# A gated cross-attention and expert layer on one core: the token work between the path walk and the softmax loop in one pass, or in four tiles of 112 tokens

## The chip, the core and the metric

The kernel runs on one core of a Trainium2 chip. The core has TensorE (PE: matrix products into the PSUM banks, and the loading of their weights), VectorE (DVE), ScalarE (ACT: activation functions with a table each), GpSimd (POOL) and SyncE (SP, which issues transfers). Each takes its own instructions in order and waits on semaphores for the others. The metric is the device time of one execution in microseconds. "Before" was run three times.

## The reference

`x` has 8 batches of 56 tokens with 128 features (448 tokens), the context 8 batches of 1500 rows. Four layers follow each other, each added to `x` with a factor `tanh(g)`:

```
x = x + tanh(g_xattn[0]) * align(context, layernorm(x))          # dynamic time warping
x = x + tanh(g_ffn[0])   * product_key_memory(layernorm(x))      # 8 heads, 1 expert each
x = x + tanh(g_xattn[1]) * attention(layernorm(x), context)      # 16 heads of 8
x = x + tanh(g_ffn[1])   * experts(layernorm(x))                 # 8 experts, best 2
```

`align` computes all distances between tokens and context rows, the cheapest warping path through them, and adds to each token the context rows that the path pairs with it. `product_key_memory` compares each token with 2 x 32 keys for each of 8 heads, takes the best key of each half (`top_k` with one final choice), and so one of 1024 rows of a table for each head: `h = gelu(x . w_down[row]) * relu(score)`, and the output is the sum of `h * w_up[row]` over the heads. Attention is `softmax(Q K^T / sqrt(8)) V` over 1500 context rows.

## The kernel before

The program has one block for each engine, written out by hand: the order of the instructions in the code is the order on the engine, and waits on named semaphores tie the engines together. TensorE's result of a step lies in a PSUM bank, of which there are eight.

Up to about 187 us the distances, the path's costs and the walk back along the path are computed, and keys and values of the context are projected; keys are split in three parts of bf16 each (key parts), stored to memory, and read back later by SyncE. What follows, up to the loop, is what the change is about:

- Path masks: for each of 4 groups of 2 batches and each of 15 context rows of a partition, ScalarE makes `Am` (`path_starts`, L692) and VectorE a mask from it (L1259), 60 of each. TensorE multiplies masks and context rows (`sums`, L1463), transposes the sums (`sums_transposed`, L1473), and VectorE adds them to `x` (`add_alignment`, L910).
- Normalization (`centre`, `scale`): TensorE makes the mean and the variance with products by a constant matrix (L1274, L1280), VectorE subtracts and squares (L860, L861), ScalarE takes the root (L715), VectorE the reciprocal and the product (L866, L867). It is done for three tiles of 112 tokens in one piece, and for the fourth in another.
- Choice of experts: similarities on TensorE (`tokens`, L1480), `choose` on VectorE (L922 to L930), which writes row numbers `idx`; GpSimd fetches the rows with 8 indirect transfers for each tile (L544). Each fetched row holds the down and the up half of an expert.
- Experts: VectorE multiplies the tokens by the fetched rows and sums (`down`, L955, L957), ScalarE applies gelu (L727), VectorE weighs the fetched up rows and sums over the heads (`up`, L962 to L965), TensorE transposes (L1512), VectorE adds (`add_memory`, L972). Another normalization follows.
- Queries: TensorE projects them (L1524), VectorE adds the bias, masks the two halves of the heads apart and splits them in three bf16 parts (L993 to L1000). TensorE lays the parts in rows with small selection matrices (L1529, 48 products), ScalarE and VectorE copy them to `QP` (L752, L1003).
- First row maxima: the scores of batch 0 for 8 pairs of heads, three products a pair (L1562), a reduction for each pair (`reduce_pair`, L1017), and a split of the maxima (L1024 to L1036), transposed (L1572) and copied (L736).
- The softmax loop, 8 batches with 12 pieces of context each: scores (L1617), exponentials (L771), weighted values (L1586), and the row maxima of the next batch (L1009). Then the expert layer (L1664, L1678).

`keep_busy` (L1314) puts products on TensorE whose results are not used. ScalarE loads another table whenever the function changes between gelu, square root and exponential.

## Time and profile before

| | before |
|---|---|
| runs, us | 537.83, 532.92, 534.33 (median 534.33) |
| profiled execution: time, span, us | 537.83, 538.0 |
| busy: PE, DVE, ACT, POOL, us | 431.0, 376.2, 263.5, 86.3 |
| mean granted clock of TensorE | 0.950 |

The profiled execution is the first of the three runs. "Span" is the time from its first to its last instruction, and the rows further down come from it. A share over the whole span says little here, since the stages have different limits; the table of windows below goes by stage.

### The profile page before, as it was taken

What the parts mean: (1) busy time and instruction counts of PE and PEld (TensorE: products, weight loads), DVE (VectorE), ACT (ScalarE), POOL (GpSimd) and SP (SyncE); (2) the same over time, 40 slices, a digit from 0 to 9 for tenths busy, and PEclk for the clock granted to TensorE, in tenths of its full rate; (3) what the DMA queues carried; (4) which work ended last, traced back from release to release, by engine and by line L of the source; (5) the groups of instructions that cost most, each with busy time, mean ns of one, the idle gap of its engine ahead of it and who ended that gap; (6) DMA issues with size and microseconds to landing.
All of it is one profiled execution on the core that took longest, in us unless ns stands there. A gap on an engine that the chain in (4) does not pass through costs nothing.

```text
span 538.0 us, 10079 instructions
## 1 busy us (share of the span) xinstructions
PE 431.0 (80%) x3977; PEld 249.1 (46%) x3977; DVE 376.2 (70%) x979; ACT 263.5 (49%) x452; POOL 86.3 (16%) x101
## 2 busy tenths in 40 slices
PE   3998877766788878400787899999899899989997
PEld 1344433334556665100233456566566566644444
DVE  7456999999566695885685988889788784271112
ACT  4264888765422393100102456566566567634443
POOL 2000000000100003677891000210210210200000
PEclk9999999989999999755788999999999999999999
DMA  8500266422641202882270003474383382000000
GB/s 287 214 2 0 94 201 186 130 86 86 196 115 57 59 2 66 214 192 85 60 155 18 1 1 76 100 174 94 81 174 78 98 256 60 3 0 1 0 0 17
DMA packets 28718, 50.05 MB, mean 93 GB/s; under 512 B 2464, under 2 KB 18400, under 8 KB 28672
## 3 DMA queue, kind: packets, MB, share of 16 engines
q1 hardware_dynamic: 26848, 45.74, 31.4%
q0 software_dynamic: 1536, 3.67, 2.7%
q8 instruction: 31, 0.51, 0.4%
q14 instruction: 15, 0.12, 0.1%
q10 hardware_dynamic: 288, 0.00, 0.0%
HBM read 39.96 MB, written 9.45 MB: 92 GB/s over the span
## 4 chain that ended last, share of the span: by engine, by line
PE 43%; DVE 37%; issue 8%; POOL 6%; ACT 3%; DMA 2%; DVEq 0%; POOLq 0%
PE banks L1586 7%; PE banks L1562 7%; POOL arena L544 6%; PE banks L1617 5%; DVE arena L1206 5%; DVE mx L1009 4%; DVE work L1235 4%; PE banks L1664 4%; PE banks L1678 4%; DVE arena L1259 2%; PE banks L1292 2%; DVE mx L1017 2%; PE banks L1430 2%; PE banks L1296 2%; DVE work L1201 2%
## 5 line engine op out<-in xcount | busy, mean ns | idle before, releaser
L1009 DVE TENSOR_REDUCE mx<-banks 112x1 f32<-112x500 f32 x168 | 106.9, 675 | 20.2 <-PE banks L1562 20.2
L771 ACT ACTIVATE arena<-banks 128x896 f32<-128x896 f32 x96 | 87.9, 917 | 51.9 <-PE banks L1617 51.2
L1314 PE MATMUL banks<-steps,one 128*128 128x500 f16 (+1 forms) x201 | 56.5, 377 | 32.3 <-DVE hcol L957 32.3
L1586 PE MATMUL banks<-arena 128*32 128x112 f32 (+1 forms) x1536 | 57.3, 265 | 2.9 <-issue 2.0
L1562 PE MATMUL banks<-ctxT,arena 128*112 128x500 bf16 x144 | 54.6, 393 | 5.6 <-issue 1.6
L1586 PEld LDWEIGHTS banks<-arena 128*32 128x32 f32 (+1 forms) x1536 | 33.7, 109 | 24.9 <-issue 20.3
L1235 DVE SCALAR_TENSOR_TENSOR work<-twice,banks,arena 128x202 f32<-128x202 f32 x68 | 29.5, 434 | 19.3 <-PE banks L1430 19.3
L1314 PEld LDWEIGHTS banks<-steps,one 128*128 128x128 f16 x201 | 20.4, 103 | 47.2 <-issue 36.7
L1617 PEld LDWEIGHTS banks<-arena,ctxT 128*128 128x128 bf16 (+1 forms) x576 | 37.3, 104 | 10.5 <-issue 2.8
L1617 PE MATMUL banks<-arena,ctxT 128*128 128x112 bf16 (+1 forms) x576 | 41.1, 213 | 0.6 <-issue 0.6
L544 POOL DMA_INDIRECT arena<-in_w_tab,idx x32 | 33.6, 1051 | 11.6 <-issue 9.4
L1206 DVE TENSOR_TENSOR_SCAN arena<-work,arena 128x100 f32<-128x100 f32 x70 | 29.8, 426 | 7.4 <-ACT work L623 5.0
L1383 PE MATMUL banks<-wts,ctxT 128*128 128x128 f32 x192 | 33.3, 273 | 0.7 <-ACT arena L680 0.7
L638 ACT ACTIVATE arena<-banks,wts 128x375 bf16<-128x375 f32 x64 | 33.5, 582 | 0.5 <-PE banks L1353 0.5
L1353 PE MATMUL banks<-arena,minusb 128*128 128x375 bf16 x64 | 20.3, 336 | 16.6 <-ACT arena L632 13.9
L787 ACT ACTIVATE arena<-banks,wts 128x448 f32<-128x448 f32 x32 | 20.3, 634 | 23.9 <-PE banks L1664 23.8
L1383 PEld LDWEIGHTS banks<-wts,ctxT 128*128 128x128 f32 x192 | 30.5, 186 | 1.2 <-ACT arena L680 1.0
L680 ACT ACTIVATE arena<-banks 128x512 f32<-128x512 f32 (+2 forms) x32 | 14.1, 492 | 34.3 <-PE banks L1383 31.4
L1664 PE MATMUL banks<-xnT,arena 128*128 128x448 f32 x64 | 30.1, 555 | 0.0
L1346 PE MATMUL banks<-ctxT,wts 128*128 128x375 f32 x64 | 27.0, 506 | 0.8
L577 POOL TENSOR_TENSOR work<-arena,mk 128x448 f32<-128x448 f32 x7 | 6.5, 932 | 125.2 <-ACT arena L747 125.2
L1562 PEld LDWEIGHTS banks<-ctxT,arena 128*112 128x112 bf16 x144 | 18.1, 128 | 17.8 <-issue 9.7
(262 smaller groups left out, 751.6 us busy)
## 6 DMA issues: line engine op xcount, KB each, us to landing
ctxT<-key_parts SPq DMA_DIRECT2D x36, 375.0 KB, 6.4
key_parts<-arena SPq DMA_DIRECT2D x32, 281.2 KB, 2.8
ctxT<-in_ctx_T SPq DMA_DIRECT2D x12, 500.0 KB, 8.9
arena<-key_parts SPq DMA_DIRECT2D x12, 375.0 KB, 7.3
ctxT<-in_ctx_nat SPq DMA_DIRECT2D x5, 750.0 KB
arena<-in_ctx_nat SPq DMA_DIRECT2D x3, 750.0 KB
arena<-in_L_ffn_W SPq DMA_DIRECT2D x1, 2048.0 KB, 8.7
arena<-in_fold_w SPq DMA_DIRECT2D x1, 768.0 KB, 5.8
```

Source lines behind the costliest of these rows:

```text
L544: nc.gpsimd.indirect_dma_start(out=gath[:, t, h, :], out_offset=None, in_=w_tab[:, :], in_offset=bass.IndirectOffsetOnAxis(ap=idx[:, c:c + ...
L638: nc.scalar.activation(kq[m % STORES][:, x, :], ps[KBANKS[m % KRING]][:, 0:KPIECE], ACT.Identity, bias=cols[:, 1:2]).then_inc(s_kx[x], 1)
L771: nc.scalar.activation(Pt[0:rows, g % 2, :].rearrange("p (a n) -> p a n", a=2), banks[0:rows, 2 + 2 * (g % 2):4 + 2 * (g % 2), 0:HQ // 2], ...
L1009: nc.vector.tensor_reduce(mx3[:, b % 2, u // NPIECE, u % NPIECE:u % NPIECE + 1], ps[k % 2][0:2 * NJ, 0:PIECE], AX_X, ALU.max).then_inc(s_m ...
L1206: nc.vector.tensor_tensor_scan(view(R, [[1, C]], (t + 1) * SLOT + 1), m, d, R[:, (t + 1) * SLOT:(t + 1) * SLOT + 1], ALU.min, ALU.add).the ...
L1235: nc.vector.scalar_tensor_tensor(out=hit_at.rearrange("p (c k) -> p c k", k=2), in0=twice[:, :].rearrange("p (c k) -> p c k", k=2), scalar ...
L1314: nc.tensor.matmul(bank[:, 0:cols], one16[:, :], steps16[:, 0:cols], start=True, stop=True, skip_group_check=True)
L1383: last = nc.tensor.matmul(ps[VALUE_BANKS[n % 6]][0:rows, k * D:(k + 1) * D], ctxT[:, b * NI + c * P:b * NI + c * P + rows], Wv_sb, start=T ...
L1562: nc.tensor.matmul(ps[k % ring][0:2 * NJ, 0:PIECE], QP[:, u // NPIECE, b, :], KP[b % 3][:, u // NPIECE, (u % NPIECE) * PIECE:(u % NPIECE + ...
L1586: last = nc.tensor.matmul(ps[6 + b % 2][q:q + 32, o:o + 2 * NJ], vals[0:rows, v0:v0 + 32], Pt[0:rows, g % 2, 2 * t * NJ:2 * (t + 1) * NJ], ...
L1617: last = nc.tensor.matmul(bank[0:rows, o:o + 2 * NJ], KP[b % 3][:, m, c * P:c * P + rows], QP[:, m, b, :], start=True, stop=True)
L1664: nc.tensor.matmul(ps[5 + i % 2][:, 0:TOK], W1s[:, e, c * P:(c + 1) * P], xnT[:, :], start=True, stop=True).then_inc(s_h, 1)
```

## The change

Everything between the path walk and the loop is done in four tiles of 112 tokens (two batches each), and the steps of one tile are written between those of the others, on each engine:

- Masks come in pieces (22, 8, 4, 7, 4, 8, 7), and between them stand, for tile 0 to 2, the addition, the normalization and (tile 0 and 1) the choice of experts.
- Centring is one product with the matrix `cmat`, identity minus mean; squares are taken on ScalarE from the PSUM bank.
- The weighted sum of the up rows goes to TensorE: for each head a product of the fetched rows with a diagonal matrix of the weights, eight of them added in one bank. The diagonals are made on ScalarE (tile 0: half of them on VectorE). Gelu, roots and diagonals of the tiles alternate on ScalarE, with a `warm_up` (a one-column activation) ahead of each change of function.
- The split of the queries goes to ScalarE and TensorE: a part is copied as bf16, and taken off in the bank by a product with the negative identity. Query rows are made for each tile; for tiles 0 and 1 ahead of the loop, for tile 2 in its batch 0, and for tile 3 in its batches 2 and 3.
- The eight `pair_scores` and `reduce_pair` of batch 0 stand between the steps of the tiles.
- The buffers of the fetched rows are placed anew: tiles 1 and 3 share one, so that the last eight fetches wait for the up products of tile 1; tile 0 lies in the place of batch 1's key parts, tile 2 in that of batch 2's. Key parts of batch 0 are loaded after the path sums, as before, those of batch 1 after the up products of tile 0, those of batch 2 after tile 2's.
- GpSimd makes the selection matrices (before on VectorE) ahead of the fetches; the memset of `QP`'s unused rows is gone, products take 96 or 99 rows in its place.
- Of the fillers between the walk and the loop, twelve become four behind the value projection, and those between the steps here become 1 to 4 in five places, ten in all.

```diff
-            for t in range(4):
+            def gather(t):
                 pool.wait_ge(s_idx, t + 1)
                 for h in range(NHK):
...
+            gather(0)
+            gather(1)
+            gather(2)
+            pool.wait_ge(s_oT, 2)
+            gather(3)
             pool.wait_ge(s_ex, NB // 2)
-            nc.gpsimd.memset(ctxT[NPR:P, 0:2 * KPW], 1.0 + 0x3F80 / 2.0 ** 23).then_inc(s_one, 1)
...
+            ones_rows(0)
+            ones_rows(1)
+            pool.wait_ge(s_oT, 3)
+            ones_rows(2)
...
+            def squares_of(t):
+                lo, hi = TILE[t]
+                act.wait_ge(s_mean, t + 3)
+                nc.scalar.activation(xsq[:, lo:hi], ps[SUM_BANK[t]][:, CEN], ACT.Square).then_inc(s_cen, 1)
...
+            def diagonals(t):
+                act.wait_ge(s_c, t + 1)
+                if t >= 1:
+                    act.wait_ge(s_oT, t)
+                for h in range(0 if t else DVE_HEADS, NHK):
+                    nc.scalar.activation(diag[:, h, :], ident[0:TT, 0:TT], ACT.Copy, scale=hcol[:, t, h:h + 1]
+                                         ).then_inc(s_dg, 1)
...
+            warm_up(ACT.Gelu)
+            gelu(1)
+            diagonals(1)
+            warm_up(ACT.Sqrt)
+            memory_squares(1)
+            memory_deviation(1)
+            for x in range(3):
+                query_part(1, x)
...
-                def up(t):
-                    ve.wait_ge(s_gelu, t + 1)
-                    link(nc.vector.tensor_tensor(hcol[:, t, :], hcol[:, t, :], score[:, t, :], ALU.mult))
-                    link(nc.vector.tensor_tensor(pr, gath[:, t, :, D:], hcol[:, t, :].unsqueeze(2).broadcast_to(
-                        [TT, NHK, D]), ALU.mult))
-                    nc.vector.tensor_reduce(x_tok[:, t, :], view(prod[0:TT, :], [[1, D], [D, NHK]]), AX_X, ALU.add
-                                            ).then_inc(s_otok, 1)
...
+            def up(t):
+
+                pe.wait_ge(s_xnc, t + 1)
+                for h in range(NHK):
...
+                    last = nc.tensor.matmul(ps[MEM_BANK[t]][:, P:P + TT], gath[t][:, h, D:], diag[:, h, :],
+                                            start=(h == 0), stop=(h == NHK - 1))
                 last.then_inc(s_oT, 1)
...
+            def query_part_off(t, x):
+                lo, hi = TILE[t]
+                pe.wait_ge(s_qs, 3 * t + x + 1)
+                nc.tensor.matmul(ps[MEM_BANK[t] if t < 2 else 7][:, 0:TT], minusb[:, :], QS[:, x, lo:hi],
+                                 start=False, stop=(x == 1), skip_group_check=True).then_inc(s_qr, 1)
...
-            keep_busy(ps[7], 14)
...
+                    if b == 0 and c == 0:
+                        queries(2)
+                    if b == 0 and c in (1, 2):
+                        query_part_off(2, c - 1)
+                    if b == 0 and c in (3, 5):
+                        pe.wait_ge(s_xn2, 4)
+                        pe.wait_ge(s_qpa, 6 if c == 3 else 8)
+                        query_rows(2, c // 2 - 1)
+                    if b == 2 and c == 5:
+                        pe.wait_ge(s_dnc, 2)
+                        queries(3)
```

VectorE at the start of the stage. L1259 before, and L1038 in the changed kernel, are the masks; L922 and L1070 begin the choice of experts. Before:

```order
L1259 SCALAR_TENSOR_TENSOR arena<-work,rowc 100x112 [waits path_starts_ready,hops_spread_copied]
L1259 SCALAR_TENSOR_TENSOR arena<-work,rowc 100x112 [waits path_starts_ready] x29
L1259 SCALAR_TENSOR_TENSOR arena<-work,rowc 100x112 [waits path_starts_ready,rows_summed]
L1259 SCALAR_TENSOR_TENSOR arena<-work,rowc 100x112 [waits path_starts_ready] x14
L1259 SCALAR_TENSOR_TENSOR arena<-work,rowc 100x112 [waits path_starts_ready,rows_summed]
L1259 SCALAR_TENSOR_TENSOR arena<-work,rowc 100x112 [waits path_starts_ready] x14
L910 SCALAR_TENSOR_TENSOR xT<-banks,gt,xT 128x336 [waits sums_transposed,gates_ready]
```

And in the changed kernel, to the last instruction of tile 0's choice:

```order
L1038 SCALAR_TENSOR_TENSOR arena<-work,rowc 100x112 [waits path_starts_ready,hops_spread_copied]
L1038 SCALAR_TENSOR_TENSOR arena<-work,rowc 100x112 [waits path_starts_ready] x21
L1051 SCALAR_TENSOR_TENSOR xT<-banks,gt,xT 128x112 [waits sums_transposed,gates_ready]
L1038 SCALAR_TENSOR_TENSOR arena<-work,rowc 100x112 [waits path_starts_ready] x8
L1058 RECIPROCAL rstd<-rstd 128x112 [waits deviation_ready]
L1059 TENSOR_TENSOR xnT<-banks,rstd 128x112 [waits dve_done]
L1038 SCALAR_TENSOR_TENSOR arena<-work,rowc 100x112 [waits path_starts_ready,rows_summed]
L1038 SCALAR_TENSOR_TENSOR arena<-work,rowc 100x112 [waits path_starts_ready] x3
L1070 TENSOR_REDUCE mxs<-banks 112x16 [waits similarities_ready]
L1071 TENSOR_TENSOR work<-banks,mxs 112x512 [waits dve_done]
L1077 TENSOR_TENSOR work<-work 112x512 [waits attention_tables_step,dve_done]
L1078 TENSOR_REDUCE ixs<-work 112x16 [waits dve_done]
```

The first choice stands behind 34 masks and no longer behind 60.

VectorE between the third tile's dot products and the loop, in the changed kernel: L1134 is a reduction of a pair's scores, L1089 and L1091 are the dot products of a tile, L1096 its weights, L1109 the addition of its outputs, L1115 and L1116 its second normalization.

```order
L1115 RECIPROCAL rstd<-rstd 128x112 [waits memory_deviation_ready]
L1116 TENSOR_TENSOR xnT<-banks,rstd 128x112 [waits dve_done]
L1089 TENSOR_TENSOR work<-arena,x_tok 112x1024 [waits rows_gathered2,tokens_copied]
L1091 TENSOR_REDUCE hcol<-work 112x8 [waits dve_done]
L1134 TENSOR_REDUCE mx<-banks 112x3 [waits row_scores_ready,expert_dots_ready]
L1096 SCALAR_TENSOR_TENSOR hcol<-score,hcol 112x8 [waits expert_gelu_ready]
L1134 TENSOR_REDUCE mx<-banks 112x3 [waits row_scores_ready]
L1109 SCALAR_TENSOR_TENSOR xT<-banks,gt,xT 128x112 [waits memory_output_ready]
L1134 TENSOR_REDUCE mx<-banks 112x3 [waits row_scores_ready]
```

The reductions, which before stood eight in a row behind the last query copy (L1017), stand one or two at a time between the steps of the tiles.

TensorE at the same place: L1663 are up products, L1723 the scores of a pair, L1670 the centring, L1676 the variance, L1682 the query projection, L1688 a part taken off, L1697 query rows.

```order
L1663 MATMUL banks<-work,arena 128x112 [waits weight_diagonals_by_act,tokens_copied]
L1663 MATMUL banks<-work,arena 128x112 [waits weight_diagonals_by_act] x7
L1723 MATMUL banks<-ctxT,arena 112x500 [waits row_scores_reduced] x3
L1670 MATMUL banks<-xT,cmat 128x112 [waits hidden_state_updated]
L1723 MATMUL banks<-ctxT,arena 112x500 [waits row_scores_reduced] x3
L1676 MATMUL banks<-xsq,meanw 128x112 [waits memory_squares_ready]
L1682 MATMUL banks<-xnT,wts 128x112 [waits memory_normalized_ready]
L1688 MATMUL banks<-work,minusb 128x112 [waits queries_split] x2
L1697 MATMUL banks<-work,arena 96x112 [waits queries_split]
L1697 MATMUL banks<-work,arena 96x112 x11
```

Every score product from the third pair on waits for the reduction two pairs earlier (`row_scores_reduced`), and the steps of tile 1 wait in the same queue; before, only the query rows of the second half stood between scores.

## Rows read from the trace of the kernel before

**Rows 1.** Windows by stage: stretch, length, busy us (instructions), granted clock, DMA share, GB/s.

```profile
core 0: us, PE busy (x) PEld busy (x) DVE busy (x) ACT busy (x) POOL busy (x), PEclk, DMA share, GB/s
187.37:219.87 32.50, 25.24 (x287) 18.12 (x285) 24.71 (x74) 19.94 (x70) 7.62 (x6) 1.00 0.23 60
219.87:264.76 44.89, 10.55 (x29) 4.20 (x30) 30.76 (x47) 2.54 (x6) 35.40 (x33) 0.54 0.58 142
264.76:293.68 28.92, 21.66 (x86) 10.19 (x85) 20.88 (x25) 4.55 (x8) 19.11 (x7) 0.88 0.39 81
293.68:310.14 16.46, 13.95 (x71) 6.90 (x70) 14.49 (x15) 6.72 (x11) 0.00 (x0) 1.00 0.00 1
310.14:452.00 141.86, 132.89 (x2244) 86.87 (x2244) 118.96 (x223) 86.68 (x103) 16.55 (x30) 1.00 0.48 113
```

**Rows 2.** Chain of waits, 184 to 312 us: start, length, what ended last.

```profile
216.30 0.70 DVE mxs L922
...
219.87 1.23 POOL arena L544
...
221.41 0.93 POOL arena L544
...
232.91 2.00 POOL arena L544
...
262.03 2.63 DMA arena<-in_w_tab,idx
...
305.29 1.72 DVE mx L1017
...
310.14 0.43 PE banks L1562
```

**Rows 3.** Timeline of VectorE, masks, and two pieces at 232 us: start, length, line.

```profile
187.37 4.17 DVE L1259 SCALAR_TENSOR_TENSOR arena<-work,rowc 100x112 f32<-100x112 f32 x15 [0.52 <-ACT work L692]
191.96 12.62 DVE L1259 SCALAR_TENSOR_TENSOR arena<-work,rowc 100x112 f32<-100x112 f32 x45 [0.42 <-ACT work L692]
...
232.31 1.02 DVE L945 MEMSET arena<- 128x1152 uint32 x1 [0.30 <-DVE score L944]
233.36 1.44 DVE L948 CAST arena<-ident 128x128 bf16<-128x128 f32 x6
```

**Rows 4.** Groups by line and shape, 186 to 345 us: busy us, mean ns, idle before.

```profile
L544 POOL DMA_INDIRECT arena<-in_w_tab,idx x32 | 33.6, 1051 | 11.6 <-issue 9.4 <-DVE idx L930 2.2
L1017 DVE TENSOR_REDUCE mx<-banks 112x3 f32<-112x1500 f32 x8 | 13.3, 1715 | 1.1 <-PE banks L1562 1.0
L955 DVE TENSOR_TENSOR work<-arena,x_tok 112x1024 f32<-112x1024 f32 x4 | 4.9, 1226 | 9.9 <-DMA arena<-in_w_tab,idx 9.9
L957 DVE TENSOR_REDUCE hcol<-work 112x8 f32<-112x1024 f32 x4 | 4.9, 1220 | 0.1
L922 DVE TENSOR_REDUCE mxs<-banks 112x16 f32<-112x512 f32 x4 | 2.7, 685 | 1.3 <-PE banks L1480 1.3
L1003 DVE CAST arena<-banks 96x448 bf16<-96x448 f32 x4 | 2.5, 620 | 4.7 <-PE banks L1529 4.7
L866 DVE RECIPROCAL rstd<-rstd 128x112 f32<-128x112 f32 x2 | 1.7, 848 | 1.0 <-ACT rstd L715 1.0
L972 DVE SCALAR_TENSOR_TENSOR xT<-banks,gt,xT 128x112 f32<-128x112 f32 x1 | 0.3, 333 | 0.6 <-PE banks L1512 0.6
```

**Rows 5.** Timeline of SyncE's queue, 200 to 290 us: the key parts of batches 0 and 1.

```profile
208.86 26.83 SPq L453 DMA_DIRECT2D ctxT<-key_parts  x12
```

**Rows 6.** Timeline of ScalarE around a table load.

```profile
303.37 0.54 ACT L752 ACTIVATE arena<-banks 96x448 bf16<-96x448 f32 x1 [0.45 <-PE banks L1529]
303.93 1.28 ACT L760 ACT_TABLE_LOAD   x1
```

**Rows 7.** TensorE's clock: a window, as in rows 1, and two rows of its timeline.

```profile
221.60:262.50 40.90, 7.82 (x17) 2.92 (x18) 29.98 (x45) 2.18 (x5) 31.76 (x31) 0.50 0.60 146
...
256.83 3.49 PE L1314 MATMUL banks<-steps,one 128*128 128x500 f16 x8 [32.34 <-DVE hcol L957]
...
292.75 1.45 PE L1562 MATMUL banks<-ctxT,arena 128*112 128x500 bf16 x6 [0.76 <-ACT arena L752]
```

More of the change, by code:

```diff
@@ new lines, in _ @@
+            deviation_of(2)
+            path_starts(54, 60)
+            token_rows(2)
+            path_sums(3)
+            warm_up(ACT.Gelu)
+            gelu(0)
+            diagonals(0)
+            squares_of(3)
+            deviation_of(3)
+            memory_squares(0)
+            memory_deviation(0)
+            for x in range(3):
+                query_part(0, x)
+            token_rows(3)
+            for a in range(2):
+                query_rows(0, 0, a)
+            warm_up(ACT.Gelu)
@@ new lines, in _ @@
+            gelu(1)
[3 more added lines that the diff above has]
+            memory_deviation(1)
+            for x in range(3):
+                query_part(1, x)
+            for r in range(2):
+                for a in range(2):
+                    query_rows(1, r, a)
+            warm_up(ACT.Gelu)
+            gelu(2)
+            diagonals(2)
+            warm_up(ACT.Sqrt)
+            memory_squares(2)
+            memory_deviation(2)
+            warm_up(ACT.Gelu)
@@ L712, in deviation @@
+            gelu(3)
+            diagonals(3)
+            warm_up(ACT.Sqrt)
             def deviation(k):
@@ L1084, in attention_layer @@
                     if u == UNITS - 1:
-                        for step in range(7):
-                            ve.wait_ge(s_dve, n)
-                            split_maxima(b, step)
+                        split_all(b)
                 def add_attention(part):
@@ new lines, in query_rows @@
+            def query_rows(t, r):
+                lo, hi = TILE[t]
+                pe.wait_ge(s_qs, 3 * (t + 1))
+                for m in range(4):
+                    for x in range(3):
+                        last = nc.tensor.matmul(ps[ROW_BANKS[t][r]][0:NPR, m * TT:(m + 1) * TT],
+                                                picks[:, 4 * r + m, x, :], QS[:, x, lo:hi],
+                                                start=(x == 0), stop=(x == 2))
+                last.then_inc(s_ql, 1)
@@ new lines, in _ @@
+            sums(0, range(NS))
+            sums(1, range(0, 4))
+            sums_transposed(0)
+            sums(1, range(4, 8))
+            centred(0)
+            sums(1, range(8, 11))
+            variance(0)
+            sums(1, range(11, NS))
+            pe.wait_ge(s_fold_sb, 1)
+            tokens(0)
+            sums(2, range(0, 4))
+            sums_transposed(1)
+            keep_busy(ps[2], 1)
+            centred(1)
+            sums(2, range(4, 8))
+            variance(1)
+            sums(2, range(8, 11))
@@ new lines, in _ @@
+            tokens(1)
+            sums(2, range(11, NS))
+            pe.wait_ge(s_idx, 1)
+            sums_transposed(2)
+            centred(2)
+            sums(3, range(0, 4))
+            variance(2)
+            sums(3, range(4, 8))
+            tokens(2)
+            sums(3, range(8, NS))
+            keep_busy(ps[0], 4)
+            sums_transposed(3)
+            keep_busy(ps[0], 2)
+            centred(3)
+            up(0)
+            memory_centred(0)
+            variance(3)
+            memory_variance(0)
@@ new lines, in _ @@
+            up(1)
+            pair_scores(3)
+            memory_centred(1)
+            pair_scores(4)
+            memory_variance(1)
+            queries(1)
+            query_part_off(1, 0)
+            query_part_off(1, 1)
+            query_rows(1, 0)
+            pair_scores(5)
+            pe.wait_ge(s_qpa, 4)
+            query_rows(1, 1)
+            up(2)
+            pair_scores(6)
+            memory_centred(2)
+            memory_variance(2)
+            pair_scores(7)
+            pe.wait_ge(s_qpa, 6)
```

666 lines of the change are left out of this document (386 added, 280 removed).

## The prediction, made before the changed kernel was run

> **What bounds the kernel now.** I read first the table of windows, to find where the engines stand idle; then the chain of waits between the path walk and the softmax loop, to see which engine ends last there; then single timelines and the groups by line, for prices. From the first path mask at 187.37 us to the loop's first product at 310.14 us lie 122.8 us, and [rows 1] show three pieces in it. While the experts' rows are fetched (219.87 to 264.76) TensorE is busy 10.55 of 44.89 us and ScalarE 2.54: the stage is as long as GpSimd's 35.40 us of indirect fetches. Before it everything runs on one chain, after it again. The chain of waits [rows 2] has in this order: masks, sums, normalization, choice of experts at 216.30, the first fetch at 219.87, 32 fetches at a pitch of 1.24 us (0.93, and 0.31 from 221.10 to 221.41) or, with the long ones up to 262.03 + 0.93, 43.1/32 = 1.35; the last lands at 264.66, and only then do the last tile's expert outputs, the third normalization, the query split, the query rows and eight first row maxima run, until 310.14. The loop (142 us) and the expert layer (86 us) keep their work. So the change is worth what it takes from these 122.8 us, less what it adds to the loop.
>
> **The change part by part.**
> *The first fetch comes earlier.* Now it waits for all 60 masks; afterwards for 34 of them and tile 0's own steps. Masks run at 12.62/45 = 0.28 us [rows 3], so 34 end at 187.4 + 9.5 + 0.4 (the pause between the two rows) = 197.3. Tile 0's VectorE steps, in the same queue: one add 0.33, one reciprocal 0.85, one product taken as 0.33, four passes over 512 columns at 0.69 (one of them stands in the rows), two small ones 0.4 [rows 4] = 4.7, so 202.0. Their waits for TensorE and ScalarE are partly covered by masks 23 to 34; I leave 2 us, at least 0 and at most the 11.7 us between masks' end (191.96 + 12.62 = 204.58) and the choice at 216.30 now, when nothing covers them. First fetch at 204, 16 us earlier. The 32 fetches still take 43 us, the third group of eight after the third choice and the last group after tile 1's outputs, because tiles 1 and 3 share a buffer. This work is moved beside the list below.
> *What VectorE has to do until the loop* sets the new bound. Masks 16.8; for each of four tiles an add, reciprocal and product (1.5), the choice (3.3), the dot products with the fetched rows (1.23 + 1.22 = 2.45), the weights 0.2, the second add 0.33, and for three of them a second reciprocal and product (1.2) [rows 4]; half of tile 0's diagonals (448 columns, estimated 0.6 from the 1.23 of 1024 columns); two query copies (0.62 each); eight reductions of 1.72 [rows 4]. That is 16.8 + 31.1 + 3.6 + 0.6 + 1.2 + 13.7 = 67.0, and the split and transposes after them 3.1 (307.01 to 310.14, [rows 2]). What leaves VectorE are the up products, the wide splits of the query, the centring and the squares. Without one wait the loop would start at 187.4 + 0.4 + 67.0 + 3.1 = 258.
> *Uncovered waits.* Before, VectorE was busy 24.71 + 30.76 + 20.88 + 14.49 = 90.8 of 122.8 us [rows 1]; there will be 68 of it, in much shorter pieces, each behind a round trip. For one tile after its dot products: gelu and its table 1.5, weights 0.2, eight diagonals on ScalarE (0.28 each, taken like masks) 2.2, eight float32 products 1 to 2, the add 0.33, centre, square, variance, root, reciprocal and product 3, query product and two differences with three copies 3, 24 query-row products 1.5 to 3, four copies 1.5: 14 to 17 us. Meanwhile VectorE has for a tile 2.45 + 3.5 + two or three reductions, some 9 to 10. So 5 to 7 us a tile stay open for three tiles; the fourth tile's round trip is moved behind the loop's start, except for its weights. With 2 us before the first fetch and 3 for the masks' second half that is 20 to 26; I take 24. Lower end 10 (VectorE always finds other work), upper end 35 (every step serial). The loop then starts at 258 + 24 = 282, against 310.14: -28.
> *Key parts.* SyncE's loads for batches 0 and 1 went out at 208.86 and their issues last 26.83 us [rows 5]; batch 0 now goes alone and should be there by about 235, before the first scores at 236 to 238. Batch 1 follows tile 0's outputs and is needed only in the loop. I cost both at nothing; if batch 0 came 5 us late, those 5 us would show in full, since the scores are first in TensorE's queue there and tile 1's up products stand behind them.
> *Tables and fillers.* Six more activation tables are loaded. In the trace a load takes 1.28 us and starts 0.02 us after the instruction ahead of it has ended (303.91 to 303.93, [rows 6]); six are 7.7 us of ScalarE, of which three stand in a round trip, 3.8 us, counted in the 24. The Trainium skill, "ScalarE: Activation LUTs", section "What ACT_TABLE_LOAD costs", adds a drain of about 1.38 us to each and advises batching by table; by it the time would be 4 us higher, 516, but the rows show no drain.
> *Added to the loop.* Two tiles' queries now go through TensorE and ScalarE inside it: for each, one float32 product, two differences, 24 small products (2 to 3 us with their handoffs) and seven copies on ScalarE, 3.2 us. TensorE is busy 132.89 of 141.86 us there [rows 1], so I charge 3 us a tile, 6 in all; bounds 2 (ScalarE has 55 us spare) and 10. The memsets that moved on GpSimd run beside other work, and the loop waits for one of three only.
> *Sum.* -28 + 6 = -22 against the profiled execution, 538.0 us in span and 537.83 in time: 516. That execution was the slowest of the three; the median, 534.33, is 3.5 lower, and I take the change off the median: **512 us**.
>
> **The rivals.**
> *A: the waits are covered.* VectorE's queue was interleaved so that every round trip meets other work, and TensorE stays at full level. With 10 us of waits the loop starts at 268, the loop's charge is 4: 534.3 - 42 + 4 = 496. For: a reduction (1.72) fits each gap. Against: TensorE and ScalarE too take their work in order, and the gap per tile above.
> *B: TensorE falls to its lower level in the whole stage.* In the fetch stage, with TensorE busy 7.82 of 40.90 us, its granted clock was 0.50, that is 1.2 GHz, and a gap of 32.34 us preceded the eight fillers at 256.83 [rows 7]; in 293.68 to 310.14, busy 13.95 of 16.46, it was 1.00. The change drops most fillers and leaves TensorE waiting between short groups. The six scores at full level take 1.45 us [rows 7], all 24 about 5; with two tiles' query rows, 32 up products and the normalizations some 16 us at full level, twice that at half; with half of it on the path the loop starts 8 us later, 290: 520. The Trainium skill, "TensorE: Matmul & The Clock Gate", section "HAM oscillation — how this bites in real kernels", describes a kernel that falls to half speed again and again because TensorE runs dry; that speaks for B, and the trace agrees with its 0.50.
> *C: fetches are slowed by VectorE beside them.* One fetch took 2.00 us while a memset and casts ran on VectorE (232.31 and 233.36, [rows 3]), against 0.93 [rows 2]. Now VectorE is busy through all 32. If each cost 2.3 with its issue (2.00 and 0.31), all 32 would last 74 us, from 204 to 278, the last land 2.63 later, and dot products, weights, two reductions and the tail (2.45 + 0.2 + 3.4 + 3.1) start the loop at 290: 520. Against: the mean of the 32 fetches was 1.05 us [rows 4], though VectorE was busy 30.76 of the stage's 44.89 us.
> *D, slower: the eight pairs become a convoy.* A pair's scores need the reduction two pairs earlier, which stands in VectorE's queue behind dot products and normalizations of the next tile, which wait for TensorE, whose queue holds those scores ahead. From 237 there are eight such rounds. The forecast implies (282 - 3.1 - 237)/8 = 5.2 us a round. At 8.6 the loop would start at 309, and with the 6 us added the kernel is 5 us slower: from there D decides; at 10 it starts at 320: 534.3 + 10 + 6 = 550. For: 14 to 17 us of round trip and 10 of VectorE's work for about 2.7 pairs give at most 9.6 when nothing overlaps. Against: only three tiles have the round trip, and the last pairs have none of it.
> *E: no change.* The work of the stage only changes its order and the waits reach 35, with B and 10 us added to the loop: loop from 301, 534.3 - 9 + 10 = 535.
>
> **How the numbers follow.** Forecast 0.45 (506 to 518), A 0.18, B 0.19, C 0.10, D 0.04, E 0.04. Runs of this kernel differ by 5 us, so 1% (5.3 us) is what can be told from no change. Faster takes the forecast, A, B and C and loses a little of their tails: 0.91; within 1% E and part of D: 0.05; slower the rest of D: 0.04. The range has to hold the forecast, most of A, B and C: 497 to 524.
>
> **What would show it.** First fetch at 202 to 208 (before 219.87); 60 masks ended by 215 to 222; VectorE busy 66 to 70 us from the first mask to the loop, and 20 to 28 idle, most of it after 228; reductions of pairs 5 us apart on the mean; the loop's first product at 282, and the loop 4 to 8 us longer than 141.86. A granted clock near 0.5 from 220 to the loop would be B, fetches over 2 us C, pairs 8 us apart D. The forecast is wrong if the fetch of the last eight, or the key parts of batch 0, ends the chain.

## The result, and the profile after

The changed kernel takes 517.49 us (median of 4 runs, 516.55 to 519.90) against 536.08 us before (4 runs, 532.92 to 538.72, those of the first table among them). The ratio is 0.967, with a 95% interval of 0.963 to 0.971: 18.6 us or 3.3% faster. Forecast were 512 us and a range of 497 to 524. In the medians of this document a run more than 1.5% above the fastest of its kernel is left out; that is one run, of 513.63 us, in e6 below.

Its profiled execution has a span of 515.5 us. The two spans must not be subtracted: here the walk ended earlier, and the first mask ran at 182.57 us against 187.37 before, in a part that the change does not touch (the first scan of the path costs began at 30.93 against 35.25). So I compare stages, each from its own start. From the first mask to the loop's first product it was 122.77 us, and is 101.18: 21.6 less. From there to the end it was 227.86, and is 231.75: 3.9 more. Together that is 17.7 us, about what the medians say.

Windows by stage of the changed kernel (columns as in [rows 1]): to the first fetch, to the first reduction of a pair, to the end of the last one, to the loop, and a stretch of the loop as long as the one in [rows 1].

```profile
182.57:200.24 17.67, 13.46 (x154) 8.74 (x152) 14.18 (x45) 12.94 (x46) 5.31 (x12) 0.98 0.00 1
200.24:240.39 40.15, 29.83 (x188) 19.26 (x189) 28.26 (x68) 21.30 (x61) 23.91 (x24) 0.71 0.63 154
240.39:279.21 38.82, 23.46 (x94) 17.16 (x95) 21.77 (x20) 13.85 (x35) 26.72 (x16) 0.54 0.47 110
279.21:283.75 4.54, 4.20 (x23) 3.57 (x23) 1.90 (x8) 3.21 (x7) 0.80 (x1) 0.50 0.21 42
283.75:425.61 141.86, 135.65 (x2245) 90.07 (x2246) 119.26 (x218) 92.21 (x118) 16.58 (x30) 0.97 0.48 113
```

VectorE is busy 14.18 + 28.26 + 21.77 = 64.2 of the 96.6 us to the last reduction, and waits 32.4. The waits grow along the way: 3.5, 11.9, 17.0. The third number from the right, the granted clock, is 0.54 in the piece with the most waits; 0.50 is 1.2 GHz.

The chain of waits after 240 us (start, length, what ended last) shows who ends them:

```profile
240.39 1.73 DVE mx L1134
242.12 0.04 issue
242.17 1.50 PE banks L1723 x3
243.66 3.40 PE banks L1663 x16
...
258.49 1.50 PE banks L1723 x3
259.99 1.09 PE banks L1697 x12
...
261.63 0.62 ACT arena L789
262.25 0.02 issue
262.27 1.28 ACT L793
...
264.63 3.72 PE banks L1663 x16
...
278.15 3.73 PE banks L1663 x16
```

Before, the chain of this stage was GpSimd's fetches and then VectorE [rows 2]. Now it is TensorE's up products (L1663, 16 records for eight products), 3.4 to 3.7 us for a tile, the scores (L1723) and ScalarE's query copies and a table load (L789, L793).

What stood ready while it waited can be read from single timelines. TensorE, then ScalarE:

```profile
240.29 1.43 PE L1723 MATMUL banks<-ctxT,arena 96*112 96x500 bf16 x3 [3.17 <-DVE idx L1082]
242.17 1.50 PE L1723 MATMUL banks<-ctxT,arena 96*112 96x500 bf16 x3 [0.45 <-DVE mx L1134]
243.46 3.59 PE L1663 MATMUL banks<-work,arena 112*128 112x112 f32 x16
```

```profile
237.09 2.34 ACT L764 ACTIVATE work<-ident,hcol 112x112 f32<-112x112 f32 x8 [0.23 <-DVE hcol L1096]
...
261.10 1.15 ACT L789 ACTIVATE arena<-banks,rowm 96x448 bf16<-96x448 f32 x2 [1.61 <-PE banks L1697]
262.27 1.28 ACT L793 ACT_TABLE_LOAD   x1
263.56 0.20 ACT L793 ACTIVATE warm<-epsc 128x1 f32<-128x1 f32 x1
263.67 0.19 ACT L757 ACTIVATE hcol<-hcol 112x8 f32<-112x8 f32 x1
```

And VectorE, with its two longest waits of the stage:

```profile
247.09 0.33 DVE L1109 SCALAR_TENSOR_TENSOR xT<-banks,gt,xT 128x112 f32<-128x112 f32 x1 [4.98 <-PE banks L1663]
...
255.41 1.22 DVE L1091 TENSOR_REDUCE hcol<-work 112x8 f32<-112x1024 f32 x1
256.71 1.72 DVE L1134 TENSOR_REDUCE mx<-banks 112x3 f32<-112x1500 f32 x1
263.90 0.17 DVE L1096 SCALAR_TENSOR_TENSOR hcol<-score,hcol 112x8 f32<-112x8 f32 x1 [5.46 <-ACT hcol L757]
```

Tile 1's diagonals were made at 239.43; its up products stood on TensorE behind the scores of pairs 1 and 2 and began at 243.5. The scores of pair 1 had themselves waited 3.17 us for VectorE's choice of experts for tile 3 (`idx`), and those of pair 2 for the reduction of pair 0. Tile 2's dot products ended at 256.63; its gelu stood on ScalarE behind tile 1's query copies and began at 263.7. Both are instructions that could run and were not at the head of their queue.

### The profile page after: what moved, and what is told of

The parts are those of the page before. It is cut to its first block, busy times and chain, and to the rows that moved or that the text cites. A ratio compares the mean times of both kernels' runs of the same rounds, so it can differ in the third digit from the quotient of the medians.

```text
span 515.5 us, 10243 instructions
## 1 busy us (share of the span) xinstructions
PE 432.8 (84%) x4022; PEld 262.8 (51%) x4022; DVE 352.5 (68%) x960; ACT 289.1 (56%) x521; POOL 82.2 (16%) x111
## 4 chain that ended last, share of the span: by engine, by line
PE 38%; DVE 12%; issue 2%; ACT 1%; DVEq 0%
PE banks L1723 9%; PE banks L1754 8%; PE banks L1854 6%; PE banks L1918 4%; DVE mx L1219 4%; PE banks L1932 4%; PE banks L1663 2%; DVE mx L1134 1%; PE banks L1740 1%; PE banks L1881 1%; DVE npart L1147 1%; PE banks L1697 1%; DVE work L1225 1%; DVE rstd L992 1%; DVE rstd L1115 1%
## 5 line engine op out<-in xcount | busy, mean ns | idle before, releaser
L1723 PE MATMUL banks<-ctxT,arena 96*112 96x500 bf16 x144 | 59.6, 436 | 10.2 <-DVE idx L1082 3.2
L1754 PEld LDWEIGHTS banks<-arena 128*32 128x32 f32 (+1 forms) x1536 | 34.0, 109 | 23.2 <-issue 20.1
L1854 PEld LDWEIGHTS banks<-arena,ctxT 99*128 99x128 bf16 (+1 forms) x576 | 37.9, 104 | 10.4 <-issue 3.0
L1406 DVE SCALAR_TENSOR_TENSOR work<-twice,banks,arena 128x202 f32<-128x202 f32 x68 | 29.5, 434 | 18.6 <-PE banks L1590 18.6
L1854 PE MATMUL banks<-arena,ctxT 99*128 99x112 bf16 (+1 forms) x576 | 41.9, 215 | 0.0
L1377 DVE TENSOR_TENSOR_SCAN arena<-work,arena 128x100 f32<-128x100 f32 x70 | 29.8, 426 | 7.4 <-ACT work L660 5.0
L917 ACT ACTIVATE arena<-banks,wts 128x448 f32<-128x448 f32 x32 | 20.3, 634 | 23.9 <-PE banks L1918 23.8
L1474 PE MATMUL banks<-steps,one 128*128 128x384 f16 (+1 forms) x110 | 33.5, 349 | 0.0
L1723 PEld LDWEIGHTS banks<-ctxT,arena 96*112 96x112 bf16 x144 | 19.8, 142 | 21.7 <-issue 11.7
L574 POOL DMA_INDIRECT arena<-in_w_tab,idx x24 | 23.8, 990 | 23.2 <-PE banks L1663 10.4
L1513 PEld LDWEIGHTS banks<-arena,minusb 128*128 128x128 bf16 x64 | 6.1, 96 | 41.0 <-ACT arena L669 29.7
L1318 DVE SCALAR_TENSOR_TENSOR xc<-banks,wts,arena 128x448 f32<-128x448 f32 x6 | 4.1, 684 | 31.7 <-PE banks L1932 31.7
```

The costliest lines, as they stand in the source:

```text
L1377: nc.vector.tensor_tensor_scan(view(R, [[1, C]], (t + 1) * SLOT + 1), m, d, R[:, (t + 1) * SLOT:(t + 1) * SLOT + 1], ALU.min, ALU.add).the ...
L1406: nc.vector.scalar_tensor_tensor(out=hit_at.rearrange("p (c k) -> p c k", k=2), in0=twice[:, :].rearrange("p (c k) -> p c k", k=2), scalar ...
L1474: nc.tensor.matmul(bank[:, 0:cols], one16[:, :], steps16[:, 0:cols], start=True, stop=True, skip_group_check=True)
L1723: nc.tensor.matmul(ps[k % ring][0:2 * NJ, 0:PIECE], QP[0:NPR, u // NPIECE, b, :], KP[b % 3][0:NPR, u // NPIECE, (u % NPIECE) * PIECE:(u % ...
L1754: last = nc.tensor.matmul(ps[6 + b % 2][q:q + 32, o:o + 2 * NJ], vals[0:rows, v0:v0 + 32], Pt[0:rows, g % 2, 2 * t * NJ:2 * (t + 1) * NJ], ...
L1854: last = nc.tensor.matmul(bank[0:rows, o:o + 2 * NJ], KP[b % 3][0:NPR + 3, m, c * P:c * P + rows], QP[0:NPR + 3, m, b, :], start=True, sto ...
```

## The experiments

Two explanations compete for the waits: TensorE's lower level (rival B), and the order of the queues (the mechanism of rival D, in a milder form). A third is the tables. Each run has one profiled execution, and the table gives for it the stage from the first mask to the loop, the granted clock and VectorE's busy time in that stage, and the time from the loop's first product to the end, in us. The last column has the median time and the number of runs. e4 and e5 leave TensorE's, VectorE's and ScalarE's steps of the stage as they are, so their 101.1 and 101.4 us beside the 101.2 show how well a stage repeats.

| run | stage | clock | VectorE | loop to end | time (median, runs) |
|---|---|---|---|---|---|
| before | 122.8 | 0.81 | 90.8 | 227.9 | 536.1 (4) |
| changed | 101.2 | 0.68 | 66.1 | 231.8 | 517.5 (4) |
| e1_fill | 93.6 | 0.88 | 66.6 | 231.4 | 515.4 (4) |
| e2_order | 93.8 | 0.71 | 66.1 | 232.1 | 510.1 (5) |
| e3_no_tables | 96.1 | 0.73 | 66.0 | 232.9 | 514.0 (1) |
| e4_loop_free | 101.1 | 0.66 | 66.0 | 233.4 | 521.6 (1) |
| e5_late_norm | 101.4 | 0.67 | 66.3 | 230.5 | 516.4 (1) |
| e6_together | 89.9 | 0.87 | 66.5 | 234.3 | 509.4 (5) |
| e7_up_on_vector | 108.6 | 0.65 | 79.3 | 236.2 | 530.1 (1) |
| e8_pairs_last | 108.8 | 0.68 | 65.2 | 231.6 | 527.7 (1) |
| e9_masks_first | 106.2 | 0.66 | 67.0 | 232.9 | 523.6 (1) |
| e10_more_fill | 88.7 | 0.94 | 67.7 | 229.3 | 505.7 (6) |

### e1_fill: is it the clock?

```diff
-            keep_busy(ps[2], 1)
+            keep_busy(ps[2], 8)
             centred(1)
...
+            keep_busy(ps[6], 12)
             pe.wait_ge(s_idx, 4)
...
             up(1)
+            keep_busy(ps[6], 8)
             pair_scores(3)
```

> Unused products are put where TensorE waits between the tiles (8 in place of 1 before tile 1's centring, 4 in place of 2 before tile 0's query product, and 6, 12, 8, 6, 12 and 20 new ones ahead of pairs 0, 1 and 3, tile 1's query product and the up products of tiles 2 and 3). In the changed kernel the stage from the first mask to the loop lasts 101.2 us with a granted clock of 0.69, and 0.54 over its last 43. If the lower level is what the stage waits for (rival B, priced at 8 us), the granted clock goes to 0.9 or more and the stage shortens to 92 to 95 us. If the waits come from the order of the queues, the clock rises and the stage keeps 98 to 103 us, since other instructions end the waits and the fillers stand ahead of TensorE's next step.

The stage shortened by 7.6 us to 93.6, with the clock at 0.88. Its up products of tile 1, to be compared with the 3.59 us above:

```profile
243.59 1.93 PE L1663 MATMUL banks<-work,arena 112*128 112x112 f32 x16
```

So the lower level is on the path of the stage, at about the price that rival B had (8 us). The time of the whole kernel shows less of it: the profiled execution, 512.00 us, is the fastest of four, the others took 513.66 to 519.16, and the median is only 2.1 us below the changed kernel's. Where the other three lost time stays open. That fillers shorten the stage is seen again in e6 and e10.

### e2_order: is it the order?

```diff
             pair_scores(0)
+            up(1)
             pe.wait_ge(s_idx, 4)
             pe.wait_ge(s_xnc, 4)
             pair_scores(1)
             pair_scores(2)
-            up(1)
...
-            for r in range(2):
-                for a in range(2):
-                    query_rows(1, r, a)
+            for a in range(2):
+                query_rows(1, 0, a)
             warm_up(ACT.Gelu)
             gelu(2)
             diagonals(2)
+            for a in range(2):
+                query_rows(1, 1, a)
```

> Only the order of two queues changes: on TensorE tile 1's up products stand ahead of pair 1's scores and no longer behind pair 2's; on ScalarE gelu and diagonals of tile 2 stand ahead of the last two query copies of tile 1. If the stage is set by work that stands ready behind a waiting instruction (tile 1's diagonals were made at 239.4, its up products ran from 243.7 to 247.1; tile 2's dot products ended at 256.6, its gelu ran at 263.7), the stage shortens by 5 to 9 us from 101.2, to 92 to 96, with the granted clock still near 0.6. If the lower clock or ScalarE's tables set it, it shortens by less than 3.

93.8 us, 7.4 less, with the clock at 0.71: the order is on the path too, and without a filler. The median fell by 7.4 us as well. Its timelines of TensorE and ScalarE:

```profile
242.10 2.33 PE L1664 MATMUL banks<-work,arena 112*128 112x112 f32 x16 [0.50 <-ACT work L764]
```

```profile
260.32 0.19 ACT L757 ACTIVATE hcol<-hcol 112x8 f32<-112x8 f32 x1
```

Its first mask ran at 185.78, 3.21 us later than in the changed kernel. By the stage's own clock tile 1's up products end 58.6 us after the first mask (64.5 before the move), and tile 2's gelu begins after 74.5 (81.1). The two causes are not quite apart in this run: at their new place the up products took 2.33 us and no longer 3.59, at a granted clock of 1.00 there against 0.50, so some 1.3 us of the gain may be the level's.

### e3_no_tables

```diff
-                nc.scalar.activation(hcol[:, t, :], hcol[:, t, :], ACT.Gelu).then_inc(s_gelu, 1)
+                nc.scalar.activation(hcol[:, t, :], hcol[:, t, :], ACT.Copy).then_inc(s_gelu, 1)
...
-            warm_up(ACT.Gelu)
+            warm_up(ACT.Copy)
```

> Gelu is left out (a copy in its place), and so the table loads between gelu and root. By the rows (a load of 1.28 us, and nothing around it) three loads stand in a round trip: the stage of 101.2 us becomes 96 to 99. If each change also costs a drain of 1.38 us, 92 to 95. If other work hides the loads, no change.

96.1 us, 5.1 less, at the lower edge of the first expectation. Eight loads of 1.28 us, 10.3 in all, fell away in the stage; the clock also rose from 0.68 to 0.73, so the 5.1 is not the tables' alone. Whether a load has more around it than its row, the rows say directly: in the changed kernel one starts at 262.27, 0.02 us after the copy ahead of it, and the next instruction starts at 263.56, 0.01 us after it. The Trainium skill, "ScalarE: Activation LUTs", section "What ACT_TABLE_LOAD costs", has 2.66 us for a load with its drain; the trace agrees with its 1.28 for the load and shows no drain here.

### e4_loop_free and e5_late_norm: what the loop lost

e4 takes this step out of the loop, and all other query steps of tiles 2 and 3 with it:

```diff
-                    if b == 0 and c == 0:
-                        queries(2)
-                    if b == 0 and c in (1, 2):
-                        query_part_off(2, c - 1)
...
```

e5 keeps them and moves one step on VectorE:

```diff
                 add_memory(3)
-                memory_normalized(3)
...
                     reduce_scores(b, u)
+                    if k == UNITS + 5:
+                        memory_normalized(3)
```

> The queries of tiles 2 and 3 are left out of the loop (those rows are zeros, set by GpSimd while it waits). From the loop's first product to the end the changed kernel takes 231.75 us, the kernel before 227.86. If the added query work costs the 3.9 us, this run takes 227.5 to 229. If it is the start of the loop (clock at 0.65 over the first 11 us, the first reductions behind tile 3's normalization), it keeps 230.5 to 232.

> VectorE's second normalization of tile 3 stands behind the loop's first six reductions and no longer ahead of them, and tile 2's query steps come three pieces later in batch 0, with nothing left out. In the changed kernel batch 0 of the loop (from the copy of its row maxima to that of batch 1's) takes 25.4 us, before 20.2; without any query work in the loop it took 24.9. If the reductions' late start is the price (the first at 286.8, 3.0 us after the loop's first product, and a normalization of 1.2 in between), batch 0 shortens to 21.5 to 23.5 and the time from the loop's first product to the end goes from 231.75 to 228.5 to 230. If TensorE's clock at the loop's start is the price (0.65 over the first 11 us), batch 0 keeps 24.5 or more.

The loop by batches (from one copy of the row maxima on ScalarE to the next, us):

| | batch 0 | 1 | 2 | 3 | 4 | 5 | 6 |
|---|---|---|---|---|---|---|---|
| before | 20.2 | 20.1 | 19.4 | 21.2 | 20.0 | 21.1 | 19.4 |
| changed | 25.4 | 19.4 | 19.7 | 20.3 | 20.8 | 20.0 | 19.7 |
| e4_loop_free | 24.9 | 19.7 | 19.4 | 20.2 | 19.6 | 23.3 | 19.7 |
| e5_late_norm | 24.1 | 19.4 | 19.7 | 20.3 | 20.8 | 20.1 | 19.7 |
| e6_together | 22.6 | 19.4 | 19.7 | 21.0 | 19.4 | 26.0 | 19.7 |

Batch 0 alone is longer than before by more than 0.8 us, by 5.2, and without any query work by 4.7 still, so e4's first expectation fell. (Its time from loop to end, 233.4, has a pause in batch 5 in it, told below, and is no measure of the query work.) VectorE's first rows in the loop, in the changed kernel and in e5:

```profile
285.71 0.85 DVE L1115 RECIPROCAL rstd<-rstd 128x112 f32<-128x112 f32 x1 [3.47 <-ACT rstd L775]
286.60 0.27 DVE L1116 TENSOR_TENSOR xnT<-banks,rstd 128x112 f32<-128x112 f32 x1
286.79 1.25 DVE L1219 TENSOR_REDUCE mx<-banks 112x1 f32<-112x500 f32 x2
```

```profile
284.80 0.68 DVE L1218 TENSOR_REDUCE mx<-banks 112x1 f32<-112x500 f32 x1 [2.18 <-PE banks L1724]
286.11 3.70 DVE L1218 TENSOR_REDUCE mx<-banks 112x1 f32<-112x500 f32 x5 [0.63 <-PE banks L1724]
```

In the changed kernel the first reduction waits for tile 3's normalization; in e5 it doesn't, and batch 0 lost 1.3 us: 24.1, between the two expectations. The granted clock was 0.67 over the first 11 us of e5's loop. In e6 and e10 it was 1.00 there, as in the kernel before, and their batch 0 took 22.6. So of the 5.2 us 1.3 go with the normalization's place (and the later query steps, which e5 moved with it) and 1.5 with the clock; the remaining 2.4 were not taken apart.

### e6_together: do the two add up?

The edits of e2 and e5, and fillers as in e1 in other numbers (the diff shows some of them):

```diff
+            keep_busy(ps[6], 6)
             pe.wait_ge(s_idx, 3)
             pair_scores(0)
             up(1)
+            keep_busy(ps[6], 4)
...
+            keep_busy(ps[6], 6)
             up(2)
...
+            keep_busy(ps[7], 22)
             up(3)
+            keep_busy(ps[0], 6)
             maxima_to_rows(0)
             memory_centred(3)
+            keep_busy(ps[0], 4)
```

> The order of e2, fillers where TensorE waits (fewer than in e1 ahead of tile 2's, and ten more between the last up products and the loop), and the late normalization of e5. Fillers and order each took 7.5 us off the stage of 101.2. If they mend different waits, the stage becomes 86 to 89, and with the loop's head mended the kernel runs in 500 to 505 us. If both only shorten the same round trips (tile 1's up products cost 3.4 us late and 1.8 us slow at once), the stage stays at 90 to 93 and the time at 506 to 509.

89.9 us: 11.3 less, not 15. The two mend in part the same round trips, as the second expectation had it. The median, 509.4 us, is hardly better than e2's 510.1. The profiled execution (511.53 us) has a pause in its loop, told below; whether the other runs, which reach from 505.07 to 513.63, had one is not known.

### e7_up_on_vector: what the up products on TensorE are worth

```diff
+            def weighted_rows(t):
...
+                link(nc.vector.tensor_tensor(pr, gath[t][:, :, D:], hcol[:, t, :].unsqueeze(2).broadcast_to(
+                    [TT, NHK, D]), ALU.mult))
+                nc.vector.tensor_reduce(x_tok[:, t, :], view(prod[0:TT, :], [[1, D], [D, NHK]]), AX_X, ALU.add
+                                        ).then_inc(s_dgv, 1)
...
             def up(t):
...
+                nc.tensor.transpose(ps[MEM_BANK[t]][:, P:P + TT], x_tok[:, t, :], ident[0:TT, 0:TT]).then_inc(s_oT, 1)
```

> The up products alone go back to VectorE (a product of 1.22 and a sum of 1.89 us for each tile, and one transpose on TensorE), all else as in the changed kernel; the diagonals fall away. By the forecast's sum VectorE has 12.4 us more to do and the diagonals' 0.6 less, so the stage of 101.2 us would become 108 to 113 if VectorE's list sets it. If the round trips do, the path per tile changes from 0.4 + 3.7 us (first diagonal, eight products at the lower clock) to 3.2 + 0.5, and the stage keeps 98 to 103.

108.6 us, 7.4 more; VectorE has 13.2 us more to do. It lies in the range of the first expectation: though VectorE waits a third of the stage, its work still counts. Not all of it does: 5.8 of the 13.2 us fell into waits or were paid back by the products and diagonals that fell away, which this run doesn't separate. This part of the change is worth about 7 us of its 21.6. The loop took 4.4 us longer too, 3.7 of them in batches 2 and 3, where TensorE paused for 1.95 and 1.00 us; they are not counted here.

### e8_pairs_last and e9_masks_first: what the order of the change is worth

e8 on VectorE (on TensorE the eight `pair_scores` stand behind `up(3)` likewise), and e9 on VectorE (on ScalarE and TensorE all path starts and sums stand first likewise):

```diff
-                reduce_pair(0)
                 add_memory(1)
-                reduce_pair(1)
-                reduce_pair(2)
...
                 row_weights(3)
+                reduce_pair(0)
+                reduce_pair(1)
...
```

```diff
-                masks(0, 22)
+                masks(0, 60)
                 add_alignment(0)
-                masks(22, 30)
                 normalized(0)
-                masks(30, 34)
...
```

> All eight pairs' scores and reductions stand behind the last tile's steps, all else as in the changed kernel. The reductions cost 8 x 1.68 = 13.4 us in a row there. If the interleaved pairs fill waits of the tiles as the forecast's sum has it, the stage of 101.2 becomes 109 to 114. If scores and reductions in the shared queues hold the tiles up (rival D's mechanism), the tiles finish some 8 us sooner and the stage is 101 to 106.

> All 60 masks stand first on VectorE and ScalarE and all sums first on TensorE; the tiles' steps follow in the same order as in the changed kernel, which has the first fetch 17.7 us after the first mask. Here the masks end at 17.4, tile 0's chain to its choice takes about 8.5 uncovered, and the first fetch is at 26. If the forecast's first step is worth its price on the path, the stage of 101.2 us becomes 108 or more; if VectorE's list and the later round trips set the stage, tile 0's dot products (at 33.8 now) start at 39 to 40 and the stage becomes 104 to 107, the waits that the masks covered now standing open.

e8: 108.8 us, 7.6 more, just under the first expectation. The reductions then take one row of VectorE's timeline:

```profile
277.31 13.49 DVE L1134 TENSOR_REDUCE mx<-banks 112x3 f32<-112x1500 f32 x8 [5.65 <-PE banks L1723]
```

Of 13.5 us of reductions the interleaving hides 7.6 net of what it costs; the convoy of rival D costs less than it saves. e9: 106.2 us, 5.0 more, with the first fetch at 209.91, 27.1 us after the first mask (17.7 in the changed kernel). The fetches come 9.4 us later, and the loop 5.0: the second expectation.

### e10_more_fill

From e6, with more fillers at tile 0's and tile 1's second normalization and query split, and fewer ahead of tile 2's up products (tile 1's query steps and the last are shown):

```diff
+            keep_busy(ps[6], 2)
             query_part_off(1, 0)
+            keep_busy(ps[6], 2)
             query_part_off(1, 1)
+            keep_busy(ps[6], 2)
             query_rows(1, 0)
+            keep_busy(ps[6], 3)
             pair_scores(5)
...
-            keep_busy(ps[6], 6)
+            keep_busy(ps[6], 1)
             up(2)
```

> As e6, with fillers moved: two or three in each short wait of tile 0's and tile 1's second normalization and query split, and one in place of the six ahead of tile 2's up products, which stood on the chain for 2.44 us at the lower clock (0.58 from 252 to 260). If the clock at those places is what is left of rival B, the granted clock of the stage goes from 0.87 to 0.95 and the stage from 89.9 to 86.5 to 88.5; if the fillers lengthen what they cover, it stays at 89.5 to 91.

88.7 us, between the two expectations and close to the first, at a clock of 0.94, and 1.00 from 243 us to the loop. Six runs from 505.12 to 507.93, median 505.69: a ratio of 0.945 (0.942 to 0.948) to the kernel before, and its slowest run is 8.6 us below the changed kernel's fastest. What is late next shows on its TensorE:

```profile
239.21 0.81 PE L1725 MATMUL banks<-ctxT,arena 96*112 96x500 bf16 x3 [2.67 <-DMA ctxT<-key_parts]
```

The first scores wait for the key parts of batch 0, which the forecast cost at nothing. They did so in e3, e4 and e5 too, for 2.0 to 2.7 us, and e4 and e5 have the changed kernel's stage to within 0.3 us: there the wait cost nothing, since the scores of pair 1 then waited for tile 3's choice. In e10, with the later waits shortened, it stands on the chain that ended last.

## Why the prediction was right, and where it was not

- **First fetch 16.6 us after the first mask:** measured 17.7 (200.24). The masks ended at 216.5, 33.9 us after the first, where the forecast left 28 to 35. e9 shows that this step is on the path, but not at its size: 9.4 us later cost 5.0.
- **VectorE's list, 67.0 us:** measured 64.2. It had left out that some neighbouring instructions overlap: the reduction at 286.79 above starts 0.08 us before the product ahead of it has ended (286.60 + 0.27), and summed singly the list's instructions come to about 66. That it counts although VectorE waits is shown by e7.
- **Uncovered waits, 24 us: the step that was wrong in size.** Measured 32.4, and the tail 4.5 where 3.1 stood. So the stage shrank by 21.6 and not by 28: 8.4 us more of waits and 1.4 of tail, less 2.8 of work and the 0.4 us pause between the masks, which the forecast had counted apart. The forecast's prices for the round trips were those of TensorE at its full level (eight up products 1 to 2 us; measured 3.4 to 3.7), and the lower level was made a rival with a chance instead of a term of the sum. e1 takes most of the level away, and its stage is 93.6 us, against the forecast's 282 - 187.4 = 94.6; but e2 comes to 93.8 by order alone, so the excess cannot be put down to the level only. The forecast also had no price for what stands ready behind a waiting instruction. Of the round trips forecast at 14 to 17 us tile 0's, with no pair between, took 17.2 (from its dot products' end at 218.87 to the last query copies' at 236.05), and tile 1's, with the scores of six pairs in the same queue, 29.8 (232.41 to 262.25).
- **Added to the loop, 6 us:** measured 3.9, by another cause. The queries inside the loop cost 0.9 us in batches 0, 2 and 3 together (e4), little more than such batches differ between runs of the same loop; most of the rest is the loop's start: a clock of 0.64 over its first 11 us (1.00 before) and the late normalization of tile 3 (e5, e6), with 2.4 us of batch 0 not taken apart. That the loop cost 2.1 us less than the 6 covered a third of the 6.6 by which the stage fell short; this is luck, since the forecast's reason for the 6 was not the one that the runs show.
- **Key parts and tables:** in the changed kernel's profile the first scores waited for VectorE's query copies and not for key parts, as forecast; in e4 and e5 they waited for key parts without harm, and in e10 on the chain. Six more tables were loaded, as forecast; they took at most 5.1 us (e3), forecast 3.8.
- **Rival B** was given 520 us and 0.19: its mechanism was there from the first fetch on (0.98 before it), and its price in the stage was about right, 7.6 us for 8 (e1). The measured 517.5 us lie nearer to its 520 than to 512. "TensorE: Matmul & The Clock Gate" of the Trainium skill, section "HAM oscillation — how this bites in real kernels", describes a kernel whose TensorE falls to half speed again and again because it waits between short groups of products; the trace agrees, with 0.54 in the stretch from 240.39 to 279.21 us, in which TensorE's pauses before scores and up products were 2.05, 3.57 and 5.77 us. **Rival A** would have been a stage of 80.6; with clock and order both mended it is 88.7 (e10). **Rival C** fell: 24 of the fetches recorded in one group took 0.99 us each with VectorE busy beside them. **Rival E**, no change, fell with the 18.6 us.
- **Rival D** had its place right and its price too high. From the first to the last of the eight reductions pass 37.1 us, 5.3 a round, with 5.2 forecast. The order it spoke of cost 7.4 us (e2), and the interleaving still pays (e8). (Its bound of 9.6 us a round should read 10.0, by its own 17 + 10 over 2.7; and rival B's 24 scores are 5.8 us by its row of 1.45 for six, not 5. Neither changes a price.)
- **The start:** the median of before was 534.3 when the forecast was made and 536.1 with one more run, 1.8 us of the 5.5 by which 512 was low.

## What to carry to other kernels

When a stage bound by one engine is broken into short round trips, price every step of the trip at TensorE's lower level, unless the trace shows what will keep it busy between them; that is a term of the sum and no rival. Then walk each in-order queue for instructions that are ready behind one that waits: two moves of that kind, without any work saved, gave as much here as the fillers. An engine that is idle a third of a stage can still lengthen it with what it is given to do: 13.2 us more of VectorE's work cost 7.4 here.

## What the runs showed that was not expected

TensorE paused for 2.05 us in the loop's batch 5, for nothing that its timeline names, in e4 and in e6, at the end of a load of key parts. Windows of e6 before, in and after it:

```profile
383.00:387.40 4.40, 4.40 (x73) 2.90 (x71) 3.58 (x6) 2.83 (x4) 1.96 (x3) 1.00 1.05 228
387.40:389.50 2.10, 0.05 (x3) 0.01 (x1) 0.25 (x1) 0.28 (x1) 0.00 (x0) 0.93 0.96 187
389.50:400.00 10.50, 10.50 (x109) 6.53 (x108) 5.77 (x9) 3.29 (x4) 0.79 (x2) 0.53 0.02 6
```

For the next 10.5 us, in which TensorE was busy throughout, the granted clock was 0.53, and the batch took 26.0 us where 20.0 is usual: here a pause of 2 us cost 6. It did not always: in e4 the batch took 23.3. And such pauses are not confined to these two runs. TensorE's rows after the longest ones of e6, of e7 and of the kernel before:

```profile
389.49 0.59 PE L1756 MATMUL banks<-arena 128*32 128x112 f32 x5 [2.05 <-issue]
```

```profile
351.02 0.39 PE L1754 MATMUL banks<-arena 128*32 128x112 f32 x6 [1.95 <-issue]
```

```profile
382.14 0.37 PE L1562 MATMUL banks<-ctxT,arena 128*112 128x500 bf16 x1 [1.65 <-issue]
```

After the pauses of 1.95 and 1.65 us the granted clock stayed at 1.00. The profile has one hint at what paused TensorE, in the list of DMA queues. Between 380 and 390 us of e6 one transfer of the queue that it calls `instruction` falls in the window from 386.8 to 388.0 us (packets, MB, share of 16 engines), while the key parts fill the engines:

```profile
q1 hardware_dynamic: 101, 0.26, 100.1%
q8 instruction: 1, 0.02, 6.4%
```

All eight such pauses of more than 1.00 us in the loops of the twelve profiles follow a transfer of this queue that ran while the DMA engines were full, and TensorE goes on 1.4 to 1.7 us after its end; but not every transfer of that kind is followed by a pause. A late load of TensorE's instructions would fit; no run moves it, so the cause stays open.

The other surprise is the start of the program: the first mask came between 182.57 and 187.37 us in the twelve profiled executions, though no edit reaches that part: 4.8 us, about as much as the runs of one kernel differ. Two spans are compared by stages for that reason.
